# Row gathers of a fused attention and expert kernel: last homes in dead token rows, and waits on the home alone

## The reference

```python
x = x + _L0_attn_ref(_layernorm(x), Wq, Wk, Wv, Wo, gw, sw)
x = x + _L0_xattn_ref(_layernorm(x), ctx, ctx, ..., rpe, ln_w, ln_b, itok_SxS2_0_2016)
x = x + _L0_ffn_ref(_layernorm(x), ...)
...
pos_emb = rpe[hops]                                    # hops is 256 x 256
pe = pos_emb.reshape(Sq, Sq, NH, DH)                   # 8 heads of 32
k_hop = jnp.einsum('bhvc,vmhc->bhvm', qh, pe)
qk = jnp.einsum('bhsd,bhtd->bhst', qh, k_scaled)
C = (qk + k_hop) * D                                   # D: decay from gates, a running maximum
h = (C / normalizer) @ vh
```

## Time and profile before

| | |
|---|---|
| median of 3 runs | 756.69 us (755.54 to 757.63) |
| the profiled execution, its own time | 752.56 us |
| its span, first to last instruction | 750.5 us |
| PE busy | 716.7 us (95%) |
| POOL busy | 444.2 us (59%) |
| DVE busy | 399.0 us (53%) |
| ACT busy | 361.6 us (48%) |
| granted TensorE clock, mean | 0.996 of full |

### The profile page before, as it was taken

One profiled execution on the slowest core, in us unless ns is written; L12 is line 12 of the kernel. 1 busy time (PEld: TensorE's weight loads), 2 busy tenths in 40 slices (PEclk: granted clock), 3 DMA queues, 4 the chain that ended last, 5 costly groups with the idle time before them and its releaser, 6 DMA issues.

```text
span 750.5 us, 17158 instructions
## 1 busy us (share of the span) xinstructions
PE 716.7 (95%) x5856; PEld 647.4 (86%) x5857; DVE 399.0 (53%) x1000; ACT 361.6 (48%) x936; POOL 444.2 (59%) x508
## 2 busy tenths in 40 slices
PE   7899999979999999979999879999999999999996
PEld 4677777859999999978999667999999999999995
DVE  3467777675756443335999993333333333333331
ACT  2444444344766444436999444444434444353441
POOL 6777777776777777775676401445454444544442
PEclk9999999999999999999999999999999999999999
DMA  8444444443333375543998993121222222122221
GB/s 294 134 119 136 130 132 140 135 127 93 95 101 104 105 235 139 154 131 104 275 260 207 305 380 143 29 42 35 35 35 38 38 35 35 35 35 40 37 35 22
DMA packets 75812, 88.29 MB, mean 118 GB/s; under 512 B 11952, under 2 KB 66032, under 8 KB 75632
## 3 DMA queue, kind: packets, MB, share of 16 engines
q0 software_dynamic: 19824, 43.93, 23.8%
q1 hardware_dynamic: 52256, 40.11, 17.9%
q10 hardware_dynamic: 3680, 3.54, 1.4%
HBM read 75.82 MB, written 11.73 MB: 117 GB/s over the span
## 4 chain that ended last, share of the span: by engine, by line
PE 77%; DVE 8%; issue 6%; POOL 4%; ACT 2%; DMA 2%; SPq 0%; DVEq 0%; POOLq 0%; ACTq 0%
PE ps L1747 19%; PE ps L1755 18%; PE ps L2053 10%; PE ps L1031 5%; POOL G L332 4%; PE ps L485 4%; PE ps L1287 2%; PE ps L552 2%; PE ps L526 2%; PE ps L478 2%; PE ps L450 1%; PE ps L1736 1%; PE ps L576 1%; PE ps L1289 1%; DMA U<-in_sw 1%
## 5 line engine op out<-in xcount | busy, mean ns | idle before, releaser
L332 POOL DMA_INDIRECT G<-in_rpe,hopi x193 | 189.7, 983 | 59.1 <-issue 52.7
L1812 ACT ACTIVATE G<-ps,U 128x128 f32<-128x128 f32 x312 | 84.9, 383 | 161.2 <-PE ps L1747 161.2
L1747 PEld LDWEIGHTS ps<-G,QT 128*128 128x128 f32 x1248 | 145.2, 192 | 1.9
L1747 PE MATMUL ps<-G,QT 128*128 128x128 f32 x1248 | 145.5, 275 | 0.0
L1755 PE MATMUL ps<-G 128*128 x624 | 141.0, 379 | 0.0
L1755 PEld LDWEIGHTS ps<-G 128*128 128x128 f32 x624 | 115.6, 190 | 14.1
L2053 PE MATMUL ps<-U,PET 128*128 128x128 f32 (+3 forms) x768 | 100.7, 275 | 0.0
L2053 PEld LDWEIGHTS ps<-U,PET 128*128 128x128 f32 x768 | 94.4, 194 | 0.1
L979 DVE COPY PET<-ps 128x512 f32<-128x512 f32 x64 | 44.2, 691 | 85.2 <-PE ps L1031 83.5
L1693 POOL DMA_INDIRECT out<-G,slots x39 | 71.4, 1830 | 23.9 <-issue 23.9
L2096 ACT ACTIVATE PET<-ps 128x512 f32<-128x512 f32 (+1 forms) x63 | 37.4, 594 | 84.7 <-PE ps L1031 81.2
(11 more groups left out here) (241 smaller groups left out, 1230.8 us busy)
## 6 DMA issues: line engine op xcount, KB each, us to landing
G<-run_max SPq DMA_DIRECT2D x16, 512.0 KB, 7.0
U<-in_w SPq DMA_DIRECT2D x16, 512.0 KB, 7.5
G<-in_w SPq DMA_DIRECT2D x8, 1024.0 KB, 12.6
G<-in_rpe,hopi POOLq DMA_INDIRECT x193, 3.0
U<-in_ctx SPq DMA_DIRECT2D x8, 256.0 KB, 2.8
tokens_kept<-X SPq DMA_DIRECT2D x8, 256.0 KB, 2.1
X<-tokens_kept SPq DMA_DIRECT2D x1, 2048.0 KB, 11.2
hidden_rows<-QT ACTq DMA_DIRECT2D x8, 256.0 KB, 7.3
```

The lines of the kernel that those rows point to most:

```text
L332: pool.indirect_dma_start(out=dst, out_offset=None, in_=rpe_d, in_offset=bass.IndirectOffsetOnAxis(ap=hopi[:, n:n + 1], axis=0)) \
L1747: mm = pe.matmul(bank(1 + 2 * u + c // 4, 4, P)[:, c % 4], w1c[u][:, k, c], hT[u][:, k, :], start=(k == 0), stop=(k == KC - 1))
L1812: ins = nc.scalar.activation(gel[u][:, c, :], bank(1 + 2 * u + c // 4, 4, P)[:, c % 4], ACT.Gelu, bias=b1c[u][:, c:c + 1])
```

## The change

The last 21 gathers get other homes: 236 to 251 go to the 16 token rows of `X`, where gathers 126 to 141 lay, and 252 to 256 to slots 65 to 69 of `G`, where 215 to 219 lay. The reload of the token rows moves on SyncE's queue from behind `turned` 71 to behind `turned` 126, after the four loads of maxima and the first context loads. In GpSimd's loop the even pace is gone: a gather waits for the last reader of its home alone, and gathers 132 to 141 wait only until the tokens that lay there are stored.

```diff
@@ rows_of(n)
+            elif n < NFIRST + NAGAIN + NBUF + NKEPT:
+                return X[:, n - NFIRST - NAGAIN - NBUF, :]
             else:
-                k = THIRD_AT + n - NFIRST - NAGAIN - NBUF
+                k = THIRD_AT + n - NFIRST - NAGAIN - NBUF - NKEPT
@@ last_in(n)
-            return NFIRST + NAGAIN + THIRD_AT + n - NFIRST - NAGAIN - NBUF
+            if n < NFIRST + NAGAIN + NBUF + NKEPT:
+                return NFULL + n - NFIRST - NAGAIN - NBUF
+            return NFIRST + NAGAIN + THIRD_AT + n - NFIRST - NAGAIN - NBUF - NKEPT
@@ mlstm_sync
             context(0)
             context(1)
+            read_until(NFIRST + NAGAIN + NBUF + NKEPT - 1)
+            sp.dma_start(X[:, 0:NKEPT, :], kept_dram).then_inc(x_ld, 16)
@@ the SyncE block
                 sp.dma_start(m_dram, r_M).then_inc(r_dma, 16)
-                sp.wait_ge(turned, (NFIRST - 1) // 2 + 1)
-                sp.dma_start(X[:, 0:NKEPT, :], kept_dram).then_inc(x_ld, 16)
                 sp.wait_ge(r_dma, 16)
@@ the GpSimd block
-                for i, n in enumerate(rest):
-
-                    evenly = NTURNED + 1 + i * (NPAIR - LEAD - NTURNED) // len(rest)
+                for n in rest:
                     if n < NFIRST:
                         pool.wait_ge(x_st, 16 * ((n - NFULL) // 2 + 1))
-                        pool.wait_ge(turned, min(evenly, n // 2 - LEAD))
                     else:
-                        pool.wait_ge(turned, max(last_in(n) // 2 + 1, min(evenly, n // 2 - LEAD)))
+                        pool.wait_ge(turned, last_in(n) // 2 + 1)
                     gather(pool, n)
```

## The result

The changed kernel takes 758.62 us (median of 20 runs, 755.79 to 760.93), the kernel before 756.71 us in the same measurement (20 runs, 754.15 to 758.25). The ratio is 1.0027, 95% interval 1.0016 to 1.0039: +1.9 us from the medians. The forecast was 759.1, slower by 2.4 us; the time lies inside its range, and the difference is just under the 0.3% that it gave as the limit of "slower". So the case that it held most likely by a little, slower by more than 0.3% (0.46), did not come, and the next one, within 0.3% (0.44), did.

A forecast was written before the change was run, and what follows sets the result against it. TensorE, busy 95% of the span, was taken as the bound, with the turning stage's end set by the last gathers. Pair 127's +0.9 us and the clock's +1.5 us made +2.4 on 756.69: 759.1 us, range 755.0 to 761.3.

The forecast's parts named there:

- The pace off gathers 132 to 141: GpSimd's loop: the one costly wait, ahead of gather 132, goes; all gathers to the last are issued 2.31 us sooner.
- B: Rival, stage's end: gathers get their share of the DMA engines beside the reload; 2.9 us won, 753.8 us; chance 0.10.
- The pace off the other gathers at nothing: GpSimd's loop: no later wait on `turned` holds GpSimd beyond its own 0.30 us per gather, so removing them costs nothing.
- The homes at nothing: Last 21 gathers: a gather into `X` moves the same 128 rows and earlier release brings nothing, so no cost.
- When the reload goes out: SyncE's queue: reload issued at about 335.8, once pair 125, started at 335.12 after waiting for gathers, is turned.
- What it does to the gathers: Stage's end: reload silences the gathers' queue from 337.8 to 340.6, catching gathers 255 and 256; pair 127 +0.9 us.
- The clock: TensorE behind its 4.4 us wait ahead of pair 127: half clock for 3.41 us costs 1.5 us, ends 0 and 3.4.
- Rival D: GpSimd's loop: something else holds gather 132, so the stream gains nothing; +4.8 us with the clock, 761.5 us; chance 0.05.
- rival C: Stage's end: reload comes later and catches gather 256 alone; about +0.5 us plus clock, 757.2 to 758.9; chance 0.12.
- Behind the stage nothing: After the last products: the reload delays nobody, the masks' earlier start wins nothing, the delay passes on whole.
- The sum: Whole kernel: +0.9 us at pair 127 and +1.5 us for the clock make +2.4 us, 759.1 us.

The follow-up runs named there:

- e7: Kernel before with the even pace taken out of GpSimd's loop, homes and reload as before: 753.4 us against 756.09 us, ratio 0.9967.
- e1: Kernel before with the even pace taken out of GpSimd's loop, homes and reload as before: 869.16 us, ratio 1.0669 to the kernel before.
- e5: Kernel before with the even pace taken out of GpSimd's loop, homes and reload as before: 871.66 us, ratio 1.0616 to the kernel before.
- e2: Changed kernel with the even pace put back, so new homes and late reload alone: 813.06 us, ratio 0.9981 to the kernel before.
- e8: Changed kernel with the even pace put back, so new homes and late reload alone: 813.14 us, ratio 0.9973 to the kernel before.
- e10: Changed kernel with four 128 x 512 matmuls without use on TensorE ahead of pair 127: 870.86 us, ratio 1.0664 to the kernel before.
- e3: Changed kernel with the reload of the token rows behind the last pair (turned 129): 868.69 us, ratio 1.0678 to the kernel before.
- e6: Changed kernel with the reload of the token rows behind the last pair (turned 129): 868.82 us, ratio 1.0580 to the kernel before.
- e9: Changed kernel with the reload of the token rows behind the last pair (turned 129): 865.23 us, ratio 1.0625 to the kernel before.
- e12: Changed kernel with the reload of the token rows behind the last pair (turned 129): 872.56 us, ratio 1.0614 to the kernel before.

## Why the prediction was right, point by point

*The pace off gathers 132 to 141, 2.31 us.* Right. Gather 132 starts 1.74 us after gather 131 in place of 4.05, which is 2.31 us, and the last gather comes 2.50 us sooner. e7 makes it a measured gain, 2.7 us in the runs and 2.64 us in the trace. For B, the price of an undisturbed stage, I had said 2.9.

*The pace off the other gathers at nothing.* Right in the conditions of the result, where e7 and the full change have 0.30 us between gathers and nobody lost by it. Wrong as a general statement: I took "no wait held GpSimd" for "the wait has no use". In e1 and e5 taking all of the pace off cost 54 and 51 us.

*The homes at nothing.* Nothing speaks against it: the issue of gathers into `X` takes 0.95 us and 0.30 us of idle time as it did into `G`, and e2 and e8 were not slower. The gathers that pair 127 waits for, 254 and 255, lie in `G` before and after. The homes were not measured by themselves where the kernel before takes 757 us.

*When the reload goes out.* Forecast: at 335.8, 163.4 us after gather 131; it was 339.09 - 176.02 = 163.1. The wait of pair 125 came as forecast too, 2.10 us.

*What it does to the gathers.* Right, and the strongest point, since the silence was read off a place where it cost nothing and came out the same 80 us later: 2.8 us, 1008 packets against 1002. Pair 127 was forecast at 342.6, 170.2 us after gather 131, and was at 170.46: +1.15 us where I had said +0.9. Two small misses stand against each other in that: from the issue of gather 255 to pair 127 it took 7.0 us in place of 6.6, and the gather was issued sooner by 2.50 us in place of 2.31. So rival B is out: a share came only after 1.03 MB. For B I had called on the Trainium skill, "DMA: Bandwidth & Descriptors", section "Queues, rings and completion order", which says that a DMA engine goes round its queue rows and switches at packet boundaries. I had read that as a fair share from the start, and the rows as disagreeing with it. The same section gives a packet up to 64 descriptors. If each 1 KB that the profile counts is one descriptor, which no run here shows, 1002 and 1008 of them over 16 DMA engines are 63 for each: an estimate, by that page's figure, of one full packet. Read so, the page and the traces do not disagree, and the error was mine. Rival D is out by gather 132, rival C by pair 127, and e7 shows that without the moved reload pair 127 is at 166.67.

*The clock, 1.5 us.* The size was right in this trace, and in part by luck: from pair 127 to the first score matmul it took 6.92 us in place of 5.24, 1.68 us more. The way there was other than written. I had one slow stretch of 3.4 us that begins behind the long wait. The trace has 10.24 us of half clock, from the short waits on, and only the last 3.5 us of it fell on work behind the wait. That these 3.5 us are so near the one stretch of 3.41 us that I had taken is chance; the moment at which the clock rose again set the price, not the length of the stretch. That this is the clock's doing is read from the records alone (eight records in 1.91 us where they took 1.06); the run that should show it, e10, did not meet the wait.

*Behind the stage nothing.* Right: 403.5 us from the first score matmul to the end, before 403.6.

*The sum.* +2.4 us forecast; the trace has 1.15 + 1.68 = +2.83, the medians +1.9. The trace is one execution, and its mean clock, 0.981, is the lowest of the 20 (0.981 to 0.989), while that of the trace of before, 0.996, is the highest that the same kernel reached in its 17 runs beside e7 (0.982 to 0.996). At full clock the same stage would be at +1.15, which may be why the medians lie between; that was not measured. One term landed elsewhere at no cost: the reload took 9.2 us in place of 11.2.

What is not shown: that a reload at another place would free the change of its loss. The full change and e7 differ in homes and reload together; the queue's silence and TensorE's wait of 4.08 us for a gather tie the 3.8 us ahead of pair 127 to the reload by the trace, not by a run of its own, and the 1.7 us behind it to the clock by the trace alone. Of all kernels tried, the pace edit alone is the fastest where the kernel before takes 757 us, and one of the slowest where it takes 815.

## What to carry to other kernels

Look in the trace for what a transfer did to others at the place where it was harmless, and carry that to the place to which it is moved: a 2 MB load that nobody noticed in the middle of a stage cost, by the trace, more than the edit beside it won, because it was issued 0.4 us before a gather for which the bound engine stood waiting. What follows from it, to start such a load early or behind the last small transfer on which the bound engine depends, is the thing to try; the second was not measured in these conditions. A wait that costs nothing in a trace is not therefore without use; before it is taken out, ask what it holds back when the engine it follows runs slower, and measure on more than one chip.

## What the runs showed of the hardware that I had not expected

- The silence is countable. In three traces (before, after, e7) the gathers' queue had at most two packets while 1.01 to 1.03 MB of a load from SyncE's queue went by in 2.8 us at 361 to 369 GB/s; after that both queues moved.
- The same program took 756 us on one chip (e7) and 815 to 821 us on four others, 8% more. On those, TensorE stood idle ahead of turns and products with no releaser that the profile shows: from 176 to 440 us for 45.9 us in e1 and 16.6 us in e8, where the traces of before and e7 show no such wait. None of the chips of the experiments was met on two occasions, so the chip and the occasion are not told apart.
- On those four chips, each kernel without the even pace (e1, e3 to e6, e9 to e12) took 865 to 873 us and each with it (e2, e8) 813 us.
- TensorE's clock may stay at 1.2 GHz while it works: in the changed kernel's profile from 8.6 to 18.9 us it was busy for 9.40 of 10.30 us at clock 0.50, and nearly all of the 3.65 us by which gather 131 was late came about there. e7's trace has 0.67 in the same stretch, before 1.00.
